# Expert stage: next rows copied and split in a block's first unit, results copied out of PSUM by VectorE, the tail's first sum by VectorE

## The reference

```python
buf = jnp.zeros((E, capacity, H), x.dtype).at[flat_e, slot].add(dispatched)
h = jax.nn.silu(jnp.einsum('ech,ehf->ecf', buf, w1))
out_buf = jnp.einsum('ecf,efh->ech', h, w2)
pair_out = out_buf[flat_e, slot] * keep[:, None].astype(x.dtype)
combined = jnp.sum(pair_out.reshape(N, K, H) * k_probs[..., None], axis=1)
return combined.reshape(B, T, H) + x        # then x = x + s * silu(this)
```

## Time and profile before

| | before |
|---|---|
| median of 3 runs | 1179.78 us |
| profiled execution | 1176.24 us |
| its span | 1173.8 us |
| busy in the span: TensorE, VectorE, ScalarE, POOL | 1003.2, 871.8, 770.8, 609.1 us |

### The profile page before, as it was taken

One profiled execution on the slowest core, in us unless ns is written; L12 is line 12 of the kernel. 1 busy time (PEld: TensorE's weight loads), 2 busy tenths in 40 slices (PEclk: granted clock), 3 DMA queues, 4 the chain that ended last, 5 costly groups with the idle time before them and its releaser, 6 DMA issues. The chain is left out here.

```text
span 1173.8 us, 18202 instructions
## 1 busy us (share of the span) xinstructions
PE 1003.2 (85%) x5032; PEld 415.3 (35%) x5032; DVE 871.8 (74%) x1795; ACT 770.8 (66%) x1460; POOL 609.1 (52%) x632
## 2 busy tenths in 40 slices
PE   4699999899999999869998999898999986888860
PEld 3123233333333332223444434344443333554530
DVE  4698889898989898847776777767675694555554
ACT  1066666676767677756876867686777754777751
POOL 5522323232323222236758777886879750465655
PEclk9999999999999999989999999999999996999995
DMA  2462825041313131479967766776676316122135
GB/s 60 80 125 70 196 74 125 15 82 24 72 31 64 40 48 44 140 206 237 232 172 218 207 197 176 200 204 180 195 212 191 114 57 253 44 56 80 56 109 216
DMA packets 102372, 149.72 MB, mean 128 GB/s; under 512 B 18216, under 2 KB 72088, under 8 KB 101838
## 3 DMA queue, kind: packets, MB, share of 16 engines
q1 hardware_dynamic: 95470, 139.65, 45.1%
q0 software_dynamic: 6272, 8.94, 2.6%
q10 hardware_dynamic: 544, 0.13, 0.2%
HBM read 109.44 MB, written 40.04 MB: 127 GB/s over the span
## 5 line engine op out<-in xcount | busy, mean ns | idle before, releaser
L766 ACT ACTIVATE a_probs<-a_score 128x512 f32<-128x512 f32 x512 | 293.1, 597 | 125.4 <-PE a_score L847 118.7
L944 DVE TENSOR_REDUCE a_mx<-a_mxps 128x2 f32<-128x1024 f32 x256 | 306.3, 1214 | 37.7 <-PE a_mxps L838 36.9
L1556 POOL TENSOR_TENSOR m_hidl<-m_hid,m_hidh 128x512 f16<-128x512 f32 x222 | 257.4, 1173 | 88.3 <-ACT m_hidh L1619 82.1
L1828 DVE TENSOR_TENSOR m_hid<-m_h,p_gates 128x512 f32<-128x512 f32 x215 | 146.9, 687 | 70.0 <-ACT m_h L1625 61.4
L1625 ACT ACTIVATE m_h<-m_h 128x512 f32<-128x512 f32 (+1 forms) x264 | 153.5, 582 | 46.2 <-PE m_h L1733 40.8
L1619 ACT ACTIVATE m_hidh<-m_hid 128x512 f16<-128x512 f32 x222 | 137.7, 620 | 45.1 <-DVE m_hid L1828 22.8
L859 PE MATMUL a_ops<-a_probs,a_vst 128*32 128x512 f32 x1024 | 136.4, 605 | 0.8 <-ACT a_probs L766 0.8
L1711 PE MATMUL m_y<-m_hidh,p_wdh 128*128 128x512 f16 (+1 forms) x264 | 100.6, 381 | 22.0 <-POOL m_hidl L1556 21.5
L2122 POOL DMA_INDIRECT t_picked<-e_yrow,p_rows x77 | 76.1, 988 | 82.8 <-DVE e_yrow L2255 61.6
L2266 DVE SCALAR_TENSOR_TENSOR e_hidl<-e_h,e_hidh 128x468 f16<-128x468 f32 (+1 forms) x96 | 57.9, 603 | 72.1 <-ACT e_hidh L2138 39.6
L847 PE MATMUL a_score<-a_qstack,a_kstack 128*128 128x512 f16 x256 | 96.9, 384 | 8.6 <-ACT a_probs L766 7.0
(11 more groups left out here) (291 smaller groups left out, 1878.4 us busy)
## 6 DMA issues: line engine op xcount, KB each, us to landing
p_gates<-t_cw SPq DMA_DIRECT2D x256, 256.0 KB
t_slots<-p_blank SPq DMA_DIRECT2D x8, 723.9 KB
p_rows<-t_slots SPq DMA_DIRECT2D x7, 723.9 KB
t_qparts<-a_qparts SPq DMA_DIRECT2D x32, 128.0 KB
t_picked<-p_blank SPq DMA_DIRECT2D x8, 512.0 KB
p_raw<-up SPq DMA_DIRECT2D x8, 512.0 KB, 4.6
p_raw<-down SPq DMA_DIRECT2D x8, 512.0 KB, 5.5
a_xin<-x SPq DMA_DIRECT2D x8, 256.0 KB, 3.3
```

Source lines behind the costliest of these rows:

```text
L766: act.activation(probs[:, kt % 2, g, :], score[:, g % 2, :], ACT.Exp, scale=SCALE / (QS * QS)).then_inc(exp_done, 1)
L944: dve.tensor_reduce(mx[ahead % 2][:, j // 2, g:g + 2], mxps[:, j % 2, :, :], AX.X, ALU.max).then_inc(mx_done, 1)
L1556: pool.tensor_tensor(hidl[0:r0, k % r, :], hid[0:r0, k % r, :], hidh[0:r0, k % r, :], ALU.subtract).then_inc(lo_done[0], 1)
L1828: dve.tensor_tensor(gated, h, gates[:, q % (SLOTS * GROUP), :], ALU.mult).then_inc(mul_done, 1)
```

## The change

In the loop, `x_high` moves to f = 0 on ScalarE, and `x_low` to f = 0 on VectorE, ahead of that unit's `e_hidl`. `result_out` moves from ScalarE (f = 3) to VectorE (f = 2), behind that unit's `e_hidl`. In the last block `result_turned(21)` and `result_rows(21)` come in f = 0, and `result_turned(22)` comes between `down(93)` and `down(94)`. In the tail the sum of piece 0 is made by VectorE and not by POOL.

```diff
-            for n in range(PIECES):
+            for n in range(1, PIECES):
                 pool.wait_ge(last_in[n], 16)
                 pool.wait_ge(base_done, n + 1)
                 pool.tensor_tensor(kept["last"][:, n, :], pick[n][:, 0, :], kept["last"][:, n, :], ALU.add
...
-            def result_out(B):
-                act.wait_ge(dn_done, FC * (B + 1))
-                if B >= 2:
-                    act.wait_ge(o_full, B - 1)
-                act.activation(yT[B % 2][:, cols(B)], yps[:, B % 2, cols(B)], ACT.Copy).then_inc(yc_done, 1)
-
...
-                if f == 1 and B + 1 < ALL:
+                if f == 0 and B + 1 < ALL:
                     x_high(B + 1)
-                if f == 3 and B:
-                    result_out(B - 1)
             high_part(FC * ALL - 1)
-            result_out(ALL - 1)
             for n in range(PIECES):
-                act.wait_ge(sum_done, n + 1)
+                if n == 0:
+                    act.wait_ge(base_done, PIECES + 1)
+                else:
+                    act.wait_ge(sum_done, n)
...
-                if f == 1 and B >= 2:
+                if f == (0 if B == ALL - 1 else 1) and B >= 2:
                     result_turned(B - 2)
-            result_turned(ALL - 2)
             for g in range(FC * ALL - XLAG, FC * ALL):
+                if g == FC * ALL - 2:
+                    result_turned(ALL - 2)
                 down(g)
             result_turned(ALL - 1)
...
+            def result_out(B):
+                dve.wait_ge(dn_done, FC * (B + 1))
+                if B >= 2:
+                    dve.wait_ge(o_full, B - 1)
+                dve.tensor_copy(yT[B % 2][:, cols(B)], yps[:, B % 2, cols(B)]).then_inc(yc_done, 1)
...
             for g in range(FC * ALL):
                 B, f = divmod(g, FC)
+                if f == 0 and B + 1 < ALL:
+                    x_low(B + 1)
+                if f == 0 and B == ALL - 1:
+                    result_rows(B - 2)
                 dve.wait_ge(hi_done, g + 1)
...
-                if f == 1 and B + 1 < ALL:
-                    x_low(B + 1)
-                if f == 1 and B >= 2:
+                if f == 1 and 2 <= B < ALL - 1:
                     result_rows(B - 2)
+                if f == 2 and B:
+                    result_out(B - 1)
             result_rows(ALL - 2)
+            result_out(ALL - 1)
             result_rows(ALL - 1)
...
+            dve.wait_ge(base_done, 1)
+            dve.wait_ge(last_in[0], 16)
+            dve.tensor_tensor(kept["last"][:, 0, :], pick[0][:, 0, :], kept["last"][:, 0, :], ALU.add).then_inc(base_done, 1)
```

## The result

| | median | lowest to highest |
|---|---|---|
| before | 1179.78 us | 1179.55 to 1183.32 |
| changed | 1173.28 us | 1169.94 to 1173.60 |

The ratio is 0.9951 (95% interval 0.9929 to 0.9973): faster by 5.8 us (3.2 to 8.4), outside the stated range of 1154 to 1168; the medians are 6.5 apart. The changed kernel's profiled execution took 1173.34 us, its span is 1171.5.

What follows compares the result with a forecast made beforehand. TensorE was taken to bound the expert stage, with holes waiting for `e_xl`. Loop 18.2, last blocks 1.6 and first sum 0.6 made 20.4 us off the median 1179.78: 1159.4 us, range 1154 to 1168.

Steps and rivals of the forecast that it cites:

- The holes: TensorE's idle before blocks' first matmuls in the loop, 22.5 us, mainly for `e_xl`; earlier `x_high` and `x_low` win most.
- The late completions: In third blocks ScalarE starts a Silu 2.1 us late; the change removes none, leaving 3.9 of 11.57 us of holes.
- Rival (a): Late completions in every loop block, about 0.6 us at 14 other gaps, losing 8.4 us: 1167.8 us; chance 0.12.
- The copy on VectorE: Result copy in the loop takes 0.635 us, slack 0.4 to 0.9; costs nothing, up to 5 us if everything slips.
- Rival (c): VectorE's result copy ends 1.0 us later, PE waits in 22 blocks, about 8 to 10 us: 1169 us; chance 0.07.
- The tail: After the loop: 1.6 us from earlier `t_last` writes in the last blocks, 0.6 from the first sum on VectorE.
- the bound of 0: Lowest gain in the last blocks: PE's wait of 1.0 grows and block 22's rows come 2 us late.
- The first sum: In the tail VectorE makes it in 0.69 us instead of POOL's 1.26, so the final chain starts 0.57 earlier.

Runs made afterwards that it cites:

- h2: Kernel before with only the result copy moved from ScalarE to VectorE, behind unit 2: 1166.55 us, ratio 0.9989.
- i3: Changed kernel without the middle one of the three up matmuls: 1171.49 us, ratio 0.9942 to the kernel before.
- i1: Changed kernel with the result copies back on ScalarE: 1177.76 us, ratio 0.9994 to the kernel before.
- i4: Changed kernel without POOL's 77 indirect writes of the first seven experts: 1144.85 us, ratio 0.9721 to the kernel before.

## Why the prediction was wrong, step by step

**The holes** were there and went, where nothing is late: no wait for `e_xl` is left but the first, and ordinary blocks take 5.00 to 5.38 us. I had sized TensorE's own work at 5.4 to 5.55 for a second block, from a record's end; it is 5.38, since the holes are deeper than the idle times by 0.16 each. My sum of the holes was too small by 23 x 0.16 = 3.7 us.

**The late completions** are the step that failed. I wrote that the change removes none of them, and then "put the recorded Silu starts through the new order" and left 3.9 us of holes. That takes lateness for a fixed delay at a fixed place. It isn't: completions are held and let go in bunches, in the changed kernel in first and second blocks too, and its six experts still take 111 to 114 us where undisturbed ones take 92.24. In the first measurement 19.0 us were lost in 20 blocks (121.65 against 102.6), not 3.9, and the last block came 7.1 us earlier and not 18.2. Behind its start I had 1.6 us won, with 0.3 set aside for lateness; 5.2 us were lost (27.5 instead of 22.3 to the writes' end). The engines still had to catch up there with late completions: block 22's unit 2 ends on TensorE at 1120.69 and is taken up at 1124.96. Loop and tail come to 17.9 of the 18.1 us by which the spans miss my 20.4. Rival (a) named it, and with too small a price: 0.6 us a gap and 1167.8, where it was 0.95 a block, single completions up to 4.35 us late, and 1173.3. "The 14 second and first blocks show none now" was read as evidence against it. That their pauses had hidden it is likely, but not shown.

**On a timely chip** the same change gives 20.4 us (1167.82 to 1147.43), which is my sum, and 19.8 on chip C. That is partly luck: of the 11.57 us behind third blocks only 7 x 0.39 = 2.7 exist there. By my steps the loop would have been 1.0 + 0.54 + 9.03 + 2.7 + 3.7 = 17.0; it is 17.5 (last block at 1103.44 instead of 1120.92). The spans of the two traces are 18.4 apart, the medians 20.4.

**The copy on VectorE**: taken at 0.635 us, and its group in the first trace of the changed kernel says so:

```profile
L2242 DVE COPY e_yT<-e_y 128x468 f32<-128x468 f32 x16 | 10.1, 633 | 0.0
```

Its cost of nothing in the loop is right on timely chips (h2). In the first measurement TensorE waits 11.7 us for it, since what VectorE and ScalarE wait for comes late; 4.27 of this is the wait in the last block that I had put at 1.0 and that is 0.70 on chip B. Rival (c) saw the wait, not the cause.

**The tail**: 1.6 + 0.6 = 2.2 predicted, 2.5 (0.9 to 4.1) measured alone. Within it, POOL's first `t_last` at 5.50 for my 5.47 and the first `t_last` load landed at 24.6 for my 24.6 are right; VectorE's sums of `t_picked` end at 22.7 for my 21.8. But I had taken the first write 1.94 us and the writes' end 1.6 us earlier than before. On chip B they are 0.9 and 1.0 earlier, since 1.0 of POOL's wait was lateness (the first write at 7.41 in the first trace, at 6.41 on chip B), and of this only 0.2 reaches SP's loads. So the traces give the tail 0.9 us and not 2.2; that the medians come near is luck. In the first measurement the tail lost 5.2 us, 3.29 of them in POOL's wait for block 22's rows: the bound of 0 was not low enough.

**The first sum**: 0.69 as priced, and ScalarE starts at once. The Trainium skill's rule on the shared port ("SBUF — State Buffer", "Who interferes with whom") wasn't tested: POOL's sum of piece 1 waited for its load until 1155.18, when VectorE's was all but over (1155.26), and took 1.26 as before. What the twenty traces do show is POOL's issues beside VectorE's sums of `t_picked`, which read two inputs in SBUF. Of 70 `t_last` issues that began while such a sum was running, 56 took 1.02 to 1.51 us, as a rule the longer the more of the sum was left; of 37 others during which one began, none took over 1.00. The sums themselves took 0.68 to 0.72 us beside an issue as alone. So POOL waits out a sum already running, and VectorE isn't held: "the two engines can hold each other up" is half right.

## What to carry to other kernels

Don't take an unexplained wait in a trace for a delay that stays where it is: shorten something else and see whether the total moves. Where a completion is taken up long after its record has ended, find what else runs in such stretches, and leave that out once. And measure a kernel on more than one chip before its gain is called 0.5% or 1.8%; here both were measured.

An idle time that is counted from the modelled end of a matmul is too short; measure a hole from start to start.

## What the runs showed of the hardware

- The same program takes 1167 to 1168 us on four chips, 1178.5 on a fifth and 1179.8 in the first measurement, whose chip isn't on record, at a granted clock of 0.97 in all. Most of the difference lies in the one stage where POOL writes rows with indirect DMAs while TensorE streams: six experts take 105.4 or 114.3 us with the kernel before, 92.2 or 110.8 to 113.6 with the changed one.
- In that stage a completion of TensorE reached an idle ScalarE up to 4.35 us after its matmul's recorded end (1009.90 to 1014.25) in the changed kernel and up to 5.60 in i3 (1063.98 to 1069.58); 0.04 us is usual. Completions are held and then let go 0.05 us apart. Without the 77 indirect writes none of the Silus' was late on chip D, and the time fell from 1172.4 to 1144.9 us.
- On chip D TensorE's granted clock in that stage was 0.91 to 0.97 in i1 to i3, and 1.00 in i4, which waits for nothing. In the first measurement it was 1.00 in the changed kernel with the same waits, so the lateness doesn't need a lower clock.
- An indirect-DMA issue of POOL usually takes 0.98 us, and up to 1.51 when it begins while VectorE adds two SBUF inputs; VectorE's sum keeps its 0.69 (70 and 37 issues in twenty traces).
